# Pairwise field products on one core: five output slots that hold a whole tile, and five stores an inner tile in place of eleven

## The chip, the core and the metric

The kernel runs on one core of one Trainium2 chip. The metric is the device time of one execution in microseconds (us), and lower is better. TensorE (PE) multiplies into PSUM, VectorE (DVE), ScalarE (ACT) and GpSimd (POOL) work on the results, and SyncE (SP) issues nearly all DMAs, which 16 DMA engines carry out.

## The reference

For each of 2048 samples there are 32 fields of 64 float32 numbers, and for each of the 496 pairs of fields (i, j), i < j, a 64x64 matrix. The output of a pair is the projection of field i times field j, element by element:

```
PAIRS = np.array(list(combinations(range(NUM_FIELDS), 2)), dtype=np.int32)
...
xi = x[:, pi, :]
xj = x[:, pj, :]
proj = jnp.einsum('bpd,pod->bpo', xi, W)
return proj * xj
```

The output is 2048 x 496 x 64 float32, 260 MB. The inputs are 17 MB of x and some 8 MB of W.

## The kernel before

**Tiles.** The 2048 samples make 16 tiles of 128 samples, one sample to a partition. Tiles are numbered 0 to 15; 0 and 15 are written out apart, 1 to 14 are the inner tiles. In a tile a pair takes 64 columns, 256 bytes of each partition, 32 KB in all.

**Steps and groups.** `plan` cuts a tile into 21 steps. A step fills two PSUM units of up to 1024 columns, `proj[b][0]` and `proj[b][1]`, and `b` alternates between the two pairs of units. Steps are gathered in 11 groups, 0 to 10, each a contiguous run of output pairs: 61, 57, 53, 49, 45, 41, 37, 33, 54, 38 and 28 pairs. Groups 0 to 9 have two steps each, group 10 has one. Between step 9 (the last of group 4) and step 10 (the first of group 5) stands the "turn": PE transposes the x of the next tile into PSUM and ACT copies it into `x_t`.

**Engines.** PE projects (L288). DVE multiplies unit 0 by x straight out of PSUM into the output slot `staged` (L330), and for a third of the steps unit 1 too. For the other steps (`pool_steps`) ACT copies unit 1 into the slot (L254) and POOL multiplies it there in place (L228). PE may overwrite a unit when DVE or ACT has emptied it.

**Slots.** `staged` is a set of nine buffers in SBUF. Groups 0 to 8 have one each; group 9 shares the buffer of group 4, and group 10 that of group 5 (`SHARED_SLOTS`). Before DVE or ACT writes a group, `slot_free` waits until the last store out of its buffer has landed. For groups 0 to 8 that is a store of the tile before (of the same group, or for slots 4 and 5 of groups 9 and 10); for groups 9 and 10 it is the store of group 4 or 5 of the same tile.

**SP.** SP's program is a fixed order. For each tile it waits for each group in turn (the last unit emptied, and POOL done) and issues its store: 11 stores, L182. Then it issues the load of the x of the tile after next into the `x_sb` that this tile has just left (`load_x`, L187). This load stands in the queue behind all stores of the tile, and the turn of the next tile waits for it: the turn in tile t reads the x of tile t+1, which was asked for at the end of tile t-1. Tiles 14 and 15 issue no such load. All of these DMAs run through one queue on the same 16 engines, and a DMA of 128 rows gives each engine 8 rows and a semaphore write.

**Descriptor area.** The program is built with the default area of SBUF for DMA descriptors, 16 KB of each partition; no DMA of this kernel is issued by POOL, which is the engine that would use it.

Of the kernel before, what the change touches and what calls it, by code (L numbers as in the profile page):

```python
# [12 lines left out]
TURN_BEFORE = 10  # L13
WARM_UP = 16

SHARED_SLOTS = {9: 4, 10: 5}


def pair_index(i, j, fields):
# [51 lines left out]
def field_pair_project(nc, x, w, ident, out, fields, dim):  # L71
# [30 lines left out]
    slot_of = [SHARED_SLOTS.get(g, g) for g in range(len(groups))]  # L102
    slots = len(groups) - len(SHARED_SLOTS)
    assert sorted(set(slot_of)) == list(range(slots))
    slot_uses = [slot_of.count(k) for k in range(slots)]
    slot_pairs = [max(group_range(g)[1] for g in range(len(groups)) if slot_of[g] == k) for k in range(slots)]


    ends = {s: max(w_at[i] + (j - i - 1 + n) * dim for i, j, n in steps[s][0]) for s in range(len(steps))}
# [15 lines left out]
    with ExitStack() as ctx:  # L125
# [9 lines left out]

        x_t = [sb(f"x_t{h}", [P, fields // 2, P]) for h in range(2)]
        ident_sb = sb("ident_sb", [P, P])
        staged = [sb(f"staged{k}", [P, slot_pairs[k] * dim]) for k in range(slots)]
# [13 lines left out]

        block = ctx.enter_context(nc.Block())

        def slot_free(eng, tile, g):

            k = slot_of[g]
            before = [h for h in range(g) if slot_of[h] == k]
            if not (tile.first and not before):
                eng.wait_ge(stored[k], tile.number * 16 * slot_uses[k] + 16 * len(before))  # L160

        def staged_part(s, i, j, n):
            g = group_of[s]
            to = (pair_index(i, j, fields) - group_range(g)[0]) * dim
            return staged[slot_of[g]][:, to:to + n * dim]

        @block.sync
        def _(sp):
            def emit(tile):
                where = {item: (b, use) for item, b, use in items(tile)}  # L170
                for g, group in enumerate(groups):
                    first, n = group_range(g)


                    pooled = any(s in pool_steps for s in group)
                    if pooled and g == 0:
                        sp.wait_ge(pool_scaled[g], tile.number + 1)
                    b, use = where[group[-1]]
                    sp.wait_ge(emptied[b][group[-1] not in pool_steps], use + 1)
                    if pooled and g > 0:  # L180
                        sp.wait_ge(pool_scaled[g], tile.number + 1)  # L181
                    sp.dma_start(out[bass.ds(tile.number * P, P), first * dim:(first + n) * dim],  # L182
                                 staged[slot_of[g]][:, 0:n * dim]).then_inc(stored[slot_of[g]], 16)

            def load_x(tile):

                sp.dma_start(x_sb[tile.parity][:], x[bass.ds((tile.number + 2) * P, P), :]  # L187
                             ).then_inc(x_loaded[tile.parity], 16)

            half = fields * dim // 2  # L190
            sp.dma_start(x_sb[0][:, 0:half], x[0:P, 0:half]).then_inc(x_first_loaded[0], 16)
            sp.dma_start(w_sb[:, w_cuts[0]:w_cuts[1]], w[:, w_cuts[0]:w_cuts[1]]).then_inc(w_loaded[0], 16)
            sp.dma_start(x_sb[0][:, half:], x[0:P, half:]).then_inc(x_first_loaded[1], 16)
# [12 lines left out]
            with sp.Fori(0, (tiles - 4) // 2) as t:  # L206
                for tile in (Tile(2 * t + 1, 1, t), Tile(2 * t + 2, 0, t + 1)):
                    emit(tile)
                    load_x(tile)
            tile = Tile(tiles - 3, 1, tiles // 2 - 2)  # L210
            emit(tile)
            load_x(tile)
            emit(Tile(tiles - 2, 0, tiles // 2 - 1))
            emit(Tile(tiles - 1, 1, tiles // 2 - 1, last=True))
            for k in range(slots):
                sp.wait_ge(stored[k], 16 * slot_uses[k] * tiles)

        @block.gpsimd
        def _(pool):
# [16 lines left out]
        @block.scalar  # L236
        def _(act):
            act.dma_start(ident_sb[:], ident).then_inc(ident_loaded, 16)

            def turned_out(b, use, to):  # L240
                for h in range(2):
                    act.wait_ge(filled[b][h], use + 1)
                    nc.scalar.activation(x_t[to][:, h * (UNIT // P):(h + 1) * (UNIT // P), :].rearrange(  # L243
                        "p k b -> p (k b)"), proj[b][h][:], ACT.Copy).then_inc(emptied[b][h], 1)

            def emit(tile):
                for item, b, use in items(tile):
                    if item == "turn":
                        turned_out(b, use, 1 - tile.parity)
                    elif item in pool_steps:  # L250
                        (i, j, n), = steps[item][1]
                        slot_free(act, tile, group_of[item])
# [61 lines left out]
        @block.vector  # L314
        def _(dve):
            def emit(tile):
                if tile.first:
                    for h in range(2):
                        dve.wait_ge(x_first_loaded[h], 16)
                for item, b, use in items(tile):  # L320
                    if item == "turn":
                        continue
                    slot_free(dve, tile, group_of[item])
                    for h in range(2):
                        if h and item in pool_steps:
# [40 lines left out]
```

## Time and profile before

| | |
|---|---|
| time, median of 3 runs | 692.61 us (691.69 to 692.86) |
| the profiled execution | 691.5 us, of which the span of instructions is 689.7 us |
| PE, DVE, POOL, ACT busy | 595.4, 415.0, 390.7, 205.1 us |
| queue 1 (SP's) busy, share of 16 engines | 99.1% |
| moved | 285.16 MB, of it 260.05 MB written to HBM |
| mean granted TensorE clock | 0.904 of full speed |

How to read it: a busy time is the sum of an engine's instructions. The DMA share is the mean busy share of the 16 DMA engines, so one engine alone shows as 0.06. Since packets of a DMA engine can overlap, a stretch can show a little over 1. A DMA's time to landing runs from its issue to the semaphore that says all 16 engines are done. The granted clock has two levels, 1.00 (2.4 GHz) and 0.50 (1.2 GHz), and a stretch's value is their mean.

### The profile page before, as it was taken

The numbers are of one execution on the slowest core, as the hardware profiler recorded it, in microseconds if no ns is written. First come the engines' busy times: TensorE is split into PE (matmuls) and PEld (weight loads), VectorE is DVE, ScalarE is ACT, GpSimd is POOL, SyncE is SP. The second block draws the span as 40 slices with busy tenths as digits, with TensorE's granted clock in tenths as the row PEclk, the third lists the DMA queues.
The fourth block names the chain that finished last, engine by engine and source line by source line (L and its number), as shares of the span: only waits on it lengthen the run. The fifth ranks groups of instructions, "written<-read, shape, count | busy, mean of one in ns | idle before, by whom it ended". The sixth has DMA issues, their size and how long they took to land.

```text
span 689.7 us, 8297 instructions
## 1 busy us (share of the span) xinstructions
PE 595.4 (86%) x2704; PEld 370.3 (54%) x2704; DVE 415.0 (60%) x528; ACT 205.1 (30%) x257; POOL 390.7 (57%) x228
## 2 busy tenths in 40 slices
PE   6969979799797979979799797979979799797972
PEld 4636646465464646646466464645646466464541
DVE  1657647486574756646576574756647576474851
ACT  2412414233241422414233241422414224141320
POOL 0735737556473745738557474755728557374651
PEclk9988989899898997989989898998979989898995
DMA  8999999999999999999999999999999999999897
GB/s 341 398 427 425 430 428 426 426 422 428 420 427 427 419 426 394 425 421 416 428 402 429 409 430 426 412 424 411 425 425 378 422 409 424 414 431 425 362 419 310
DMA packets 29755, 285.16 MB, mean 413 GB/s; under 512 B 3312, under 2 KB 3440, under 8 KB 7216
## 3 DMA queue, kind: packets, MB, share of 16 engines
q1 hardware_dynamic: 29600, 284.96, 99.1%
q8 instruction: 5, 0.08, 0.0%
q10 hardware_dynamic: 144, 0.07, 0.0%
q14 instruction: 6, 0.05, 0.0%
HBM read 24.97 MB, written 260.05 MB: 413 GB/s over the span
## 4 chain that ended last, share of the span: by engine, by line
DMA 37%; POOL 26%; issue 22%; PE 10%; ACT 2%; DVE 1%; POOLq 0%; SPq 0%; DVEq 0%; ACTq 0%
DMA out_dram<-staged 36%; POOL staged L228 26%; PE proj L288 9%; ACT staged L254 2%; DVE staged L330 1%; DMA ident_sb<-ident_dram 1%; PE proj L305 1%; POOLq L227 0%; PE proj L266 0%; ACT x_t L243 0%; SPq L182 0%; POOLq L120 0%; ACTq L253 0%; DVEq L125 0%; SPq L181 0%
## 5 line engine op out<-in xcount | busy, mean ns | idle before, releaser
L288 PE MATMUL proj<-w_sb,x_t 64*128 64x512 f32 (+7 forms) x2432 | 561.8, 563 | 75.6 <-DVE staged L330 73.2
L330 DVE TENSOR_TENSOR staged<-proj,x_sb 128x1024 f32<-128x1024 f32 (+7 forms) x528 | 415.0, 828 | 263.8 <-PE proj L288 183.0
L228 POOL TENSOR_TENSOR staged<-staged,x_sb 128x1024 f32<-128x1024 f32 (+4 forms) x224 | 390.5, 1755 | 283.9 <-ACT staged L254 283.2
L288 PEld LDWEIGHTS proj<-w_sb,x_t 64*128 64x128 f32 x2432 | 338.4, 205 | 291.8 <-issue 134.1
L254 ACT ACTIVATE staged<-proj 128x1024 f32<-128x1024 f32 (+4 forms) x224 | 172.8, 787 | 455.5 <-PE proj L288 344.0
L243 ACT ACTIVATE x_t<-proj 128x1024 f32<-128x1024 f32 x32 | 31.0, 1021 | 10.6 <-PE proj L266 9.1
L266 PEld LDWEIGHTS proj<-ident_sb,x_sb 128*128 128x128 f32 x256 | 28.6, 143 | 8.8 <-issue 7.6
L266 PE MATMUL proj<-ident_sb,x_sb 128*128 128x128 f32 x256 | 32.2, 280 | 0.6 <-DMA x_sb<-x_dram 0.6
L305 PE MATMUL proj<-ident_sb 128*128 128x128 f32 x16 | 3.7, 421 | 5.5 <-DMA ident_sb<-ident_dram 5.5
L305 PEld LDWEIGHTS proj<-ident_sb 128*128 128x128 f32 x16 | 3.3, 223 | 5.5 <-DMA ident_sb<-ident_dram 5.5
L243 ACT ACT_TABLE_LOAD x1 | 1.3, 1283 | 1.2 <-PEq L360 1.2
L360 POOL MEMSET const-float32-0.0<- 128x1 f32 x1 | 0.1, 98 | 0.2 <-issue 0.2
L360 POOL MEMSET const-bfloat16-1.0<- 128x1 bf16 x1 | 0.1, 102 | 0.0
L360 POOL MEMSET const-uint8-127<- 128x1 uint8 x1 | 0.1, 102 | 0.0
L360 POOL MEMSET const-float32-1.0<- 128x1 f32 x1 | 0.1, 98 | 0.0
## 6 DMA issues: line engine op xcount, KB each, us to landing
out_dram<-staged SPq DMA_DIRECT2D x16, 1952.0 KB, 11.4
out_dram<-staged SPq DMA_DIRECT2D x16, 1824.0 KB, 14.1
out_dram<-staged SPq DMA_DIRECT2D x16, 1728.0 KB, 17.3
out_dram<-staged SPq DMA_DIRECT2D x16, 1696.0 KB, 14.7
out_dram<-staged SPq DMA_DIRECT2D x16, 1568.0 KB, 14.3
out_dram<-staged SPq DMA_DIRECT2D x16, 1440.0 KB, 15.6
out_dram<-staged SPq DMA_DIRECT2D x16, 1312.0 KB, 15.6
out_dram<-staged SPq DMA_DIRECT2D x16, 1216.0 KB, 12.1
```

Source lines behind the costliest of these rows:

```text
L228: last = nc.gpsimd.tensor_tensor(product, product, x_sb[tile.parity][:, j * dim:(j + n) * dim], ALU.mult)
L243: nc.scalar.activation(x_t[to][:, h * (UNIT // P):(h + 1) * (UNIT // P), :].rearrange("p k b -> p (k b)"), proj[b][h][:], ACT.Copy).then_i ...
L254: nc.scalar.activation(staged_part(item, i, j, n), proj[b][1][:, 0:n * dim], ACT.Copy).then_inc(emptied[b][1], 1)
L266: last = nc.tensor.transpose(proj[b][h][:, n * P:(n + 1) * P], x_sb[of][:, k * P:(k + 1) * P], ident_sb[:])
L288: last = nc.tensor.matmul(proj[b][h][:, at:at + width], x_t[tile.parity][half, i // 2, :], w_sb[half, col:col + width], start=True, stop=True)
L305: nc.tensor.transpose(proj[1][0][:, 0:P], ident_sb[:], ident_sb[:])
L330: last = nc.vector.tensor_tensor(staged_part(item, i, j, n), proj[b][h][:, at:at + n * dim], x_sb[tile.parity][:, j * dim:(j + n) * dim], ...
L360: nc = bacc.Bacc("TRN2", target_bir_lowering=False, num_devices=1)
```

## The change

There are now five slots, one for each of the merged runs of groups 0-1, 2-3, 4-6, 7-8 and 9-10, of 118, 102, 123, 87 and 66 pairs: 496 pairs, a whole tile, where the nine buffers held 430. No slot is used twice in a tile. The room comes from the descriptor area, cut to 1 KB of each partition.

In tiles 1 to 14 SP issues one store for each merged run, when its last group is done. Tiles 0 and 15 keep their eleven stores of one group each, which read their part of the slot. DVE and ACT wait for a slot once, at its first step (ACT: its first pool step), until the store of the tile before has landed; tile 0 waits for none, and tile 1 waits until all groups of a slot of tile 0 have landed.

```
+MERGED = [[0, 1], [2, 3], [4, 5, 6], [7, 8], [9, 10]]
+
+DMA_SCRATCH = 1024
...
+        staged = [sb(f"staged{k}", [P, n * dim]) for k, (_, n) in enumerate(slot_range)]
...
+        def slot_free(eng, tile, k):
+
+            if not tile.first:
+                eng.wait_ge(stored[k], tile.number * 16 + 16 * (len(MERGED[k]) - 1))
...
+                fine = tile.first or tile.last
+                for these in ([[g] for g in range(len(groups))] if fine else MERGED):
+                    k, g = slot_of[these[0]], these[-1]
+                    first, n = group_range(these[0])[0], sum(group_range(h)[1] for h in these)
...
+                    at = (first - slot_range[k][0]) * dim
                     sp.dma_start(out[bass.ds(tile.number * P, P), first * dim:(first + n) * dim],
-                                 staged[slot_of[g]][:, 0:n * dim]).then_inc(stored[slot_of[g]], 16)
+                                 staged[k][:, at:at + n * dim]).then_inc(stored[k], 16)
...
@@ -320,7 +324,9 @@
-                    slot_free(dve, tile, group_of[item])
+                    k = slot_of[group_of[item]]
+                    if item == groups[MERGED[k][0]][0]:
+                        slot_free(dve, tile, k)
...
+    nc = bacc.Bacc("TRN2", target_bir_lowering=False, num_devices=1,
+                   dynamic_dma_scratch_size=DMA_SCRATCH)
```

SP's program in the first tile of the loop, before: the stores of groups 0 to 8, their widths in float32 columns of a row (64 to a pair). Register instructions stand between them.

```order
L182 DMA out_dram<-staged 128x3904
L179 REGISTER_ALU
L182 ISA
L182 DMA out_dram<-staged 128x3648
L179 REGISTER_ALU
L182 ISA
L182 DMA out_dram<-staged 128x3392
L179 REGISTER_ALU
L182 ISA
L182 DMA out_dram<-staged 128x3136
```

And the same tile on SP now, from its first store to the load of x; `pool_scaled1` is POOL's signal for group 1 and `emptied` that of DVE or ACT.

```order
L184 DMA out_dram<-staged 128x7552
L180 REGISTER_ALU
L184 ISA [waits pool_scaled3,emptied00]
L184 DMA out_dram<-staged 128x6528
L180 REGISTER_ALU
L184 ISA [waits pool_scaled6,emptied10]
L184 DMA out_dram<-staged 128x7872
L180 REGISTER_ALU
L184 ISA [waits pool_scaled8,emptied11]
L184 DMA out_dram<-staged 128x5568
```

Two stores now take the place of the first four, a third that of groups 4, 5 and 6, and the load of x still comes behind the last store of the tile.

ACT's program around the turn in a tile of the loop, before (`stored` is a slot's semaphore, `filled` PE's; the two L243 rows are the copies of the turn):

```order
L253 REGISTER_ALU [waits stored4]
L254 ACTIVATE staged<-proj 128x896 [waits filled01]
L243 ACTIVATE x_t<-proj 128x1024 [waits filled10]
L243 ACTIVATE x_t<-proj 128x1024 [waits filled11]
L253 REGISTER_ALU [waits stored5]
L254 ACTIVATE staged<-proj 128x512 [waits filled01]
L253 REGISTER_ALU [waits stored6]
L254 ACTIVATE staged<-proj 128x512 [waits filled01]
L254 ACTIVATE staged<-proj 128x640 [waits filled11,stored6]
```

and the same rows now:

```order
L257 REGISTER_ALU [waits stored2]
L258 ACTIVATE staged<-proj 128x896 [waits filled01]
L245 ACTIVATE x_t<-proj 128x1024 [waits filled10]
L245 ACTIVATE x_t<-proj 128x1024 [waits filled11]
L257 REGISTER_ALU
L258 ACTIVATE staged<-proj 128x512 [waits filled01]
L257 REGISTER_ALU
L258 ACTIVATE staged<-proj 128x512 [waits filled01]
L258 ACTIVATE staged<-proj 128x640 [waits filled11]
```

The order of the work is the same; the waits for slots 5 and 6 are gone, and one wait, for the merged slot 2, stands ahead of step 9.

## Rows read from the trace of the kernel before

**Rows 1.** The page: span, DMA queue, busy engines and DMA share in 40 slices.

```profile
span 689.7 us, 8297 instructions
...
PE 595.4 (86%) x2704; PEld 370.3 (54%) x2704; DVE 415.0 (60%) x528; ACT 205.1 (30%) x257; POOL 390.7 (57%) x228
...
DMA  8999999999999999999999999999999999999897
...
q1 hardware_dynamic: 29600, 284.96, 99.1%
```

**Rows 2.** DMA issues of the page: count, KB each, median us from issue to landing.

```profile
out_dram<-staged SPq DMA_DIRECT2D x16, 1952.0 KB, 11.4
...
out_dram<-staged SPq DMA_DIRECT2D x16, 1728.0 KB, 17.3
...
out_dram<-staged SPq DMA_DIRECT2D x16, 896.0 KB, 10.5
```

**Rows 3.** Waits, whole run: total us, times, longest.

```profile
ACT staged L254 <- DMA out_dram<-staged: 111.0, 16, 9.0
...
DVE staged L330 <- DMA out_dram<-staged: 76.8, 16, 6.9
```

**Rows 4.** The chain: start, length of the pieces that end with group 4 landed.

```profile
77.22 15.10 DMA out_dram<-staged
...
616.24 15.57 DMA out_dram<-staged
```

**Rows 5.** Stretches: start:end, length, busy per engine, granted clock, DMA share, GB/s.

```profile
640.00:644.00 4.00, 4.00 (x22) 2.70 (x20) 3.02 (x3) 1.94 (x2) 2.82 (x2) 1.00 0.88 366
644.00:646.00 2.00, 2.00 (x11) 1.09 (x8) 2.00 (x3) 0.81 (x1) 2.00 (x2) 1.00 0.06 24
646.00:684.00 38.00, 26.75 (x117) 15.92 (x114) 20.46 (x29) 8.00 (x11) 19.48 (x12) 0.81 1.00 418
684.00:686.00 2.00, 0.00 (x0) 0.00 (x0) 0.00 (x0) 0.00 (x0) 0.00 (x0) 0.50 0.48 198
686.00:688.00 2.00, 0.00 (x0) 0.00 (x0) 0.00 (x0) 0.00 (x0) 0.00 (x0) 0.50 0.08 34
```

**Rows 6.** DMA queue 1 in 12:20, 71:88 and 88:98: packets, MB, share.

```profile
q1 hardware_dynamic: 668, 3.33, 101.6%
...
q1 hardware_dynamic: 597, 7.25, 100.3%
...
q1 hardware_dynamic: 481, 4.23, 99.8%
```

**Rows 7.** SP in order of time, 0:120, then group 6 with 7 (window 84:86).

```profile
0.75 0.40 SPq L191 DMA_DIRECT2D x_sb<-x_dram  x1
...
20.47 38.80 SPq L182 DMA_DIRECT2D out_dram<-staged  x11
59.32 0.46 SPq L187 DMA_DIRECT2D x_sb<-x_dram  x1
65.44 34.87 SPq L182 DMA_DIRECT2D out_dram<-staged  x11
...
84.67 1.47 SPq L182 DMA_DIRECT2D out_dram<-staged  x2
```

**Rows 8.** PE in order of time in tile 1; L266 is the turn.

```profile
73.81 1.97 PE L266 MATMUL proj<-ident_sb,x_sb 128*128 128x128 f32 x16
75.70 13.73 PE L288 MATMUL proj<-w_sb,x_t 64*128 64x512 f32 x64
93.38 15.00 PE L288 MATMUL proj<-w_sb,x_t 64*128 64x448 f32 x58 [3.94 <-DVE staged L330]
```

**Rows 9.** Stretches of the run's start and around tile 1's idle time.

```profile
0.00:5.00 5.00, 0.00 (x0) 0.00 (x0) 0.00 (x0) 1.28 (x1) 0.20 (x4) 1.00 0.56 150
...
89.00:92.00 3.00, 0.43 (x2) 0.00 (x0) 0.00 (x0) 0.00 (x0) 0.00 (x0) 1.00 1.00 426
92.00:95.00 3.00, 1.62 (x2) 0.83 (x3) 1.55 (x2) 1.19 (x2) 1.80 (x2) 0.59 1.01 429
95.00:98.00 3.00, 3.00 (x14) 2.68 (x14) 0.60 (x2) 0.00 (x0) 0.96 (x1) 0.50 1.01 427
98.00:101.00 3.00, 3.00 (x14) 1.61 (x12) 2.65 (x8) 0.38 (x1) 0.00 (x0) 0.78 1.02 434
```

More of the change, by code:

```diff
@@ L14 @@
 WARM_UP = 16
-SHARED_SLOTS = {9: 4, 10: 5}
+MERGED = [[0, 1], [2, 3], [4, 5, 6], [7, 8], [9, 10]]
+DMA_SCRATCH = 1024
 def pair_index(i, j, fields):
@@ L100, in group_range @@
         return first, sum(n for _, _, n in segments)
[L102 to L106, printed above, removed]
+    slot_of = [next(k for k, merged in enumerate(MERGED) if g in merged) for g in range(len(groups))]
+    slots = len(MERGED)
+    slot_range = [(group_range(m[0])[0], sum(group_range(g)[1] for g in m)) for m in MERGED]
     ends = {s: max(w_at[i] + (j - i - 1 + n) * dim for i, j, n in steps[s][0]) for s in range(len(steps))}
@@ L137, in field_pair_project @@
         ident_sb = sb("ident_sb", [P, P])
-        staged = [sb(f"staged{k}", [P, slot_pairs[k] * dim]) for k in range(slots)]
+        staged = [sb(f"staged{k}", [P, n * dim]) for k, (_, n) in enumerate(slot_range)]
         proj = [[ctx.enter_context(nc.psum_tensor(f"proj{b}{h}", [P, UNIT], F32)) for h in range(2)]
@@ L153, in field_pair_project @@
         block = ctx.enter_context(nc.Block())
[L155 to L160, printed above, removed]
+        def slot_free(eng, tile, k):
+            if not tile.first:
+                eng.wait_ge(stored[k], tile.number * 16 + 16 * (len(MERGED[k]) - 1))
         def staged_part(s, i, j, n):
-            g = group_of[s]
-            to = (pair_index(i, j, fields) - group_range(g)[0]) * dim
-            return staged[slot_of[g]][:, to:to + n * dim]
+            k = slot_of[group_of[s]]
+            to = (pair_index(i, j, fields) - slot_range[k][0]) * dim
+            return staged[k][:, to:to + n * dim]
         @block.sync
@@ L170, in emit @@
                 where = {item: (b, use) for item, b, use in items(tile)}
[L171 to L181, printed above, removed]
+                fine = tile.first or tile.last
+                for these in ([[g] for g in range(len(groups))] if fine else MERGED):
+                    k, g = slot_of[these[0]], these[-1]
+                    first, n = group_range(these[0])[0], sum(group_range(h)[1] for h in these)
+                    pooled = [h for h in these if any(s in pool_steps for s in groups[h])]
+                    if pooled and these[0] == 0:
+                        sp.wait_ge(pool_scaled[pooled[-1]], tile.number + 1)
+                    b, use = where[groups[g][-1]]
+                    sp.wait_ge(emptied[b][groups[g][-1] not in pool_steps], use + 1)
+                    if pooled and these[0] > 0:
+                        sp.wait_ge(pool_scaled[pooled[-1]], tile.number + 1)
+                    at = (first - slot_range[k][0]) * dim
                     sp.dma_start(out[bass.ds(tile.number * P, P), first * dim:(first + n) * dim],
-                                 staged[slot_of[g]][:, 0:n * dim]).then_inc(stored[slot_of[g]], 16)
+                                 staged[k][:, at:at + n * dim]).then_inc(stored[k], 16)
             def load_x(tile):
@@ L215, in _ @@
             for k in range(slots):
-                sp.wait_ge(stored[k], 16 * slot_uses[k] * tiles)
+                sp.wait_ge(stored[k], 16 * (tiles - 2 + 2 * len(MERGED[k])))
         @block.gpsimd
@@ L251, in emit @@
                         (i, j, n), = steps[item][1]
-                        slot_free(act, tile, group_of[item])
+                        k = slot_of[group_of[item]]
+                        if item == min(s for s in pool_steps if slot_of[group_of[s]] == k):
+                            slot_free(act, tile, k)
                         act.wait_ge(filled[b][1], use + 1)
@@ L322, in emit @@
                         continue
-                    slot_free(dve, tile, group_of[item])
+                    k = slot_of[group_of[item]]
+                    if item == groups[MERGED[k][0]][0]:
+                        slot_free(dve, tile, k)
                     for h in range(2):
@@ L359 @@
     }
-    nc = bacc.Bacc("TRN2", target_bir_lowering=False, num_devices=1)
+    nc = bacc.Bacc("TRN2", target_bir_lowering=False, num_devices=1,
+                   dynamic_dma_scratch_size=DMA_SCRATCH)
     aps = [nc.dram_tensor(n, a.shape, F32, kind="ExternalInput").ap() for n, a in arrays.items()]
```

## The prediction, made before the changed kernel was run

> **What bounds the kernel now.** I read the page first. The DMA queue is busy for 99.1% of the span, and all 40 slices but the first, the last and one near the end show a 9, while the busiest compute engine, PE, has 86% [rows 1]. So the kernel is bound by its transfers, and the question about any edit is what it does to the DMA engines' own time. Next, the waits. ACT and DVE each wait once a tile for a store to land, 111.0 and 76.8 us in 16 waits [rows 3]: compute is ahead and stands still until the shared buffer of group 9 is free. That waiting is a result of the bound and its removal is worth nothing by itself.
>
> Then the chain of waits, which has one long DMA piece a tile. It ends where group 4's store lands: at 77.22 + 15.10 = 92.32 us in tile 1 and at 616.24 + 15.57 = 631.81 in tile 14 [rows 4]. So a tile takes 539.49 / 13 = 41.50 us. It moves 496 pairs and one x, as much as 528 pairs of 32 KB, 17.30 MB.
>
> The stretches near the end say which DMA engine that is. At 644 to 646 us the DMA share is 0.06, one engine of 16: fifteen had run out of work and one had not. After the last work of the others the same is seen, 0.48 and then 0.08 [rows 5]. One engine is behind, and since a store has landed only when all 16 are done, that one sets the slots' release and the end. For it the queue isn't empty at any time that the rows show.
>
> **What a packet costs.** Three undisturbed stretches with rows of different length give it [rows 6]. Queue 1's busy time is share x 16 x length: 130.0 us for 668 packets (195 ns each, 4985 bytes) in 12:20, 272.8 us for 597 (457 ns, 12144 bytes) in 71:88, 159.7 us for 481 (332 ns, 8794 bytes) in 88:98. Each two of the three give a line: 0.0366, 0.0373 and 0.0361 ns a byte, and 12.0, 3.9 and 15.0 ns a packet whatever its size. I take their mean, about 10 ns, and keep 3.9 and 15 as bounds. As a check, a tile for an average engine: 17.30 MB / 16 x 0.0366 = 39.6 us, plus 12 DMAs x 9 packets (8 rows and a semaphore) x 10 ns = 1.1 us, 40.7 us in all. The 41.50 us of the chain are the slow engine's; 0.8 us a tile are its own.
>
> **The change, part by part.**
>
> Fewer stores. Tiles 1 to 14 issue 5 stores in place of 11, so 14 x 6 = 84 stores go, and with each 9 packets on every engine; the bytes stay. The slow engine saves 84 x 9 x 10 ns = 7.6 us (2.9 us at 3.9 ns, 11.3 at 15). All of it lies on the path, because that engine has no gap. SP's issuing of 84 stores goes too, and is worth nothing: SP waits for compute.
>
> On this the Trainium skill speaks twice (DMA: Bandwidth & Descriptors). Its Rules for kernel authors ask for 128 partitions and at least 1 MiB a DMA; all stores but that of group 10 (896 KB) fulfil it already [rows 2], and who stops there gets nothing for the merging. Its section Why small descriptors are slow gives a packet about three cycles of 32 bytes and 32 bytes of descriptor, 128 bytes in all; at 0.0366 ns a byte that is an estimate of 4.7 ns a packet and 3.6 us for the change. The rows above give a greater sum, so the trace does not agree with the size.
>
> The slow engine's 0.8 us a tile. No row says whether it pays them by bytes or by rows. By bytes nothing changes, and that is what I take, since the other 39.6 of its 41.5 us go by bytes too. By rows, 48 of 96 go and so does half: 0.4 x 14 = 5.6 us more gain. If long rows are dearer for it, it loses instead; a like amount the other way, up to 0.5 us a tile, 7 us, is my bound above.
>
> Slots. Each slot's use is a whole tile apart, so groups 9 and 10 wait for nothing of their own tile and the stall of rows 3 goes from its place. Compute doesn't get further ahead by much, since the next thing is late: the turn. The turn in tile t needs the x issued at the end of tile t-1, behind all of that tile's stores. Before, it never waited noticeably: in tile 1 it ran at 73.81 [rows 8] with x issued at 59.32 [rows 7]. Now compute is some groups further ahead when the queue reaches that x, so I expect PE to wait at the turn in each of tiles 1 to 14. Behind that wait stands everything of PE, and so groups 5 to 10 on all engines.
>
> Coarser issue. What covers this wait is what is already in the queue when x lands: merged runs 0 and 1 of the tile, 118 + 102 = 220 pairs. Group 4 is computed but can't be issued, since its run ends with group 6. At the new pace, 41.0 us for 528 pairs, the cover is 17.1 us. Within that time the turn, group 5 and group 6 must be done. In tile 1 before, from the turn's start at 73.81 [rows 8] to the issue of group 6 at 84.67 [rows 7] it took 10.9 us, all at clock 1.00 (2.4 GHz). After a stall of 3.9 us PE restarted at 93.38 [rows 8] and was granted 0.50 (1.2 GHz) until about 99.3, 5.9 us [rows 9]. Half of these 5.9 us is lost, so the way takes 10.9 + 3.0 = 13.9 us. From issue to first packet I allow 1.4 us: SP's first DMA issued at 0.75 [rows 7], and a share of 0.56 over the first 5 us [rows 9] means packets from 2.2 us on. 13.9 + 1.4 = 15.3 us against 17.1: the DMA engines don't run dry, with 1.8 us to spare. This is the thinnest number here. Once run 2 is issued there are 123 pairs of it, 9.6 us, to cover groups 7 and 8, and the rest of the tile is looser still.
>
> Other places cost nothing. A merged run 0 in tile 1 is issued later than group 0 was, but the stores of tile 0 cover it: the store of group 0 of tile 0 was issued at 20.47 and x at 59.32 [rows 7], and the queue was then busy to 71 us and beyond. Without the wait of group 9, tile 0 is done some 8 us sooner. At the end, tile 15 has its fine stores and group 10's as the last, as before, and one engine that ends after the others.
>
> **The sum.** The profiled execution took 691.5 us; less 7.6 gives 683.9. It lies 1.1 us under the median of 692.61, so the forecast for a median is 692.6 - 7.6 = **685.0 us**.
>
> **Rivals.**
>
> 1. The turn's wait isn't covered, slower. The place is the way from the turn to the issue of run 2, and the mechanism the granted clock. For it: there are 1.8 us to spare, and after every stall the clock was 0.50 for about 6 us; in the turn the small transposes may keep it there longer. Were it low on the whole way, 10.9 us of PE's work would take up to 21.7. From 17.1 - 1.4 = 15.7 us on, each us costs 14 us, so at 16.3 us the change is as slow as before (14 x 0.6 = 8.4 eats the gain of 7.6). With the clock low for 12 us the way takes 16.9 and the time is 692.6 - 7.6 + 14 x 1.2 = 702 us. Against it: in rows 9 the clock came back in full while PE had much to do, which holds behind the turn as well. Chance 0.08.
>
> 2. The slow engine pays by rows: 692.6 - 7.6 - 5.6 = 679.4 us. Chance 0.09.
>
> 3. Long rows are dearer for the slow engine. Its 0.8 us grow by 0.5 a tile, 7 us, and the time is 692.0, no change. For it: rows of up to 31 KB are twice as long as any in the trace. Against it: the three stretches lie on nearly one line from 5 to 12 KB. Chance 0.07.
>
> 4. The change doesn't do what it says. Rows over 16 KB are cut in two, so the packets come back and only the 84 semaphore writes go, 84 x 10 ns = 0.8 us: 691.8 us, no change. Nothing in the trace shows a row cut, but the longest is 15.6 KB. The Trainium skill's ≥1 MiB rule would give the same, by another way: a store's cost is amortized already. Against that stands the 10 ns line of rows 6. Chance 0.06.
>
> **How the numbers follow.** The forecast has 0.70, with its own range of 681.3 to 689.7 from the bounds of a packet. The range that holds 8 in 10 takes in the case of 679.4 and the edge of the forecast's upper side, 679.0 to 690.5; outside are 702, the two cases near 692 and a little of the rest. A measurement of this kernel tells 0.2%, 1.4 us, from no change. Faster by more than that is everything under 691.2: 0.70 + 0.09, and a little of cases 3 and 4, **0.80**. Within 0.2%: **0.12**. Slower: **0.08**.
>
> **What would show it.** Right: queue 1 has 84 x 144 = 12096 packets fewer, 17504 in place of 29600; from one tile to the next 41.0 us in place of 41.50; ACT and DVE no longer wait for a store in each tile, and PE waits about 4 us at the turn for the load of x, with clock 0.50 behind it; the DMA share stays at 0.98 or more, and at the end one engine is left alone. Wrong: a DMA share that falls once a tile to 0 between run 1 and run 2 (rival 1), a period under 40.7 us (rival 2), or 41.5 us with the fewer packets (rival 3) or as many packets as before (rival 4). If 84 stores less take off under 3 us with no dip in the share, the 10 ns of a packet were wrong.

## The result, and the profile after

The changed kernel is slower. Its median is 696.74 us (6 runs, 695.55 to 698.52) against 691.79 us for the kernel before (6 runs on the same chip, 691.28 to 692.86): a ratio of 1.0071, 95% interval 1.0061 to 1.0081. The forecast was 685.0 us, faster. The profiled execution took 697.26 us with a span of 695.5.

The page of the changed kernel has these rows; the last two parts are the chain by engine and the DMA issues (count, KB each, median us from issue to landing):

```profile
span 695.5 us, 7741 instructions
...
PE 577.8 (83%) x2704; PEld 364.4 (52%) x2704; DVE 410.6 (59%) x528; ACT 208.5 (30%) x257; POOL 391.6 (56%) x228
...
DMA  8999999999999999999999999999999999999997
...
q1 hardware_dynamic: 17504, 284.96, 98.9%
...
PE 44%; DMA 43%; DVE 6%; SPq 2%; issue 1%; ACT 0%; DVEq 0%; ACTq 0%
...
x_sb<-x_dram SPq DMA_DIRECT2D x15, 1024.0 KB, 19.6
```

The 12096 packets are gone, exactly as forecast, and the bytes are the same. The queue is as busy as before, 98.9% against 99.1% [rows 1], and its 40 slices show nothing. By this view the kernel has fewer packets, the same bytes and the same busy share, and yet takes longer. So the time of some packets must have grown.

The waits (total us, times, longest) show where compute stands now:

```profile
ACT x_t L245 <- PE proj L270: 114.2, 31, 7.9
...
PE proj L270 <- DMA x_sb<-x_dram: 83.0, 15, 6.2
```

No wait for a store is left on ACT or DVE; those of rows 3 are gone. In their place PE waits at the turn for x, 5.5 us on average, as forecast (about 4). The chain of waits (start, length) gives the period from one turn to the next:

```profile
53.80 18.20 DMA x_sb<-x_dram
72.05 3.68 PE proj L270 x16
...
178.30 19.56 DMA x_sb<-x_dram
197.90 3.67 PE proj L270 x16
...
618.02 3.68 PE proj L270 x16
```

(618.02 - 72.05) / 13 = 42.00 us a tile, where 41.50 was measured before [rows 4] and 41.0 was forecast. In the chain the load of x now stands where group 4's store stood.

Last, stretches (columns as in rows 5) behind one turn, and at the end of the run:

```profile
197.00:211.00 14.00, 12.84 (x55) 8.62 (x57) 6.02 (x8) 4.42 (x6) 4.07 (x3) 0.76 0.98 420
...
665.00:689.00 24.00, 5.52 (x32) 3.72 (x29) 5.76 (x11) 1.43 (x3) 4.89 (x3) 0.71 1.01 424
689.00:692.00 3.00, 0.00 (x0) 0.00 (x0) 0.00 (x0) 0.00 (x0) 0.00 (x0) 0.50 0.79 327
692.00:695.50 3.50, 0.00 (x0) 0.00 (x0) 0.00 (x0) 0.00 (x0) 0.00 (x0) 0.50 0.07 29
```

Behind the turn the granted clock is 0.76 on average for 14 us, and the DMA share is 0.98: what was feared there, a queue that runs empty, hardly happens.

### The profile page after: what moved, and what is told of

The parts are those of the page before. It is cut to its first block, busy times and chain, and to the rows that moved or that the text cites. A ratio compares the mean times of both kernels' runs of the same rounds, so it can differ in the third digit from the quotient of the medians.

```text
span 695.5 us, 7741 instructions
## 1 busy us (share of the span) xinstructions
PE 577.8 (83%) x2704; PEld 364.4 (52%) x2704; DVE 410.6 (59%) x528; ACT 208.5 (30%) x257; POOL 391.6 (56%) x228
## 3 DMA queue, kind: packets, MB, share of 16 engines
q1 hardware_dynamic: 17504, 284.96, 98.9%
## 4 chain that ended last, share of the span: by engine, by line
PE 44%; DMA 43%; DVE 6%; SPq 2%; issue 1%; ACT 0%; DVEq 0%; ACTq 0%
DMA x_sb<-x_dram 43%; PE proj L292 37%; PE proj L270 8%; DVE staged L336 6%; SPq L197 1%; SPq L184 1%; SPq L189 0%; ACT staged L258 0%; SPq L201 0%; SPq L195 0%; SPq L194 0%; SPq L193 0%; DVEq L333 0%; DVEq L126 0%; ACTq L257 0%
## 5 line engine op out<-in xcount | busy, mean ns | idle before, releaser
L336 DVE TENSOR_TENSOR staged<-proj,x_sb 128x1024 f32<-128x1024 f32 (+7 forms) x528 | 410.6, 827 | 261.9 <-PE proj L292 259.3
L292 PE MATMUL proj<-w_sb,x_t 64*128 64x512 f32 (+7 forms) x2432 | 521.0, 536 | 4.0 <-DVE staged L336 2.6
L292 PEld LDWEIGHTS proj<-w_sb,x_t 64*128 64x128 f32 x2432 | 311.9, 190 | 207.8 <-issue 126.7
L270 PE MATMUL proj<-ident_sb,x_sb 128*128 128x128 f32 x256 | 54.4, 401 | 83.0 <-DMA x_sb<-x_dram 83.0
L270 PEld LDWEIGHTS proj<-ident_sb,x_sb 128*128 128x128 f32 x256 | 49.2, 215 | 92.2 <-DMA x_sb<-x_dram 92.2
L245 ACT ACTIVATE x_t<-proj 128x1024 f32<-128x1024 f32 x32 | 32.6, 1024 | 114.2 <-PE proj L270 114.2
## 6 DMA issues: line engine op xcount, KB each, us to landing
out_dram<-staged SPq DMA_DIRECT2D x14, 2112.0 KB, 17.1
out_dram<-staged SPq DMA_DIRECT2D x2, 1952.0 KB, 16.1
```

The costliest lines, as they stand in the source:

```text
L270: last = nc.tensor.transpose(proj[b][h][:, n * P:(n + 1) * P], x_sb[of][:, k * P:(k + 1) * P], ident_sb[:])
L292: last = nc.tensor.matmul(proj[b][h][:, at:at + width], x_t[tile.parity][half, i // 2, :], w_sb[half, col:col + width], start=True, stop=True)
L336: last = nc.vector.tensor_tensor(staged_part(item, i, j, n), proj[b][h][:, at:at + n * dim], x_sb[tile.parity][:, j * dim:(j + n) * dim], ...
```

## Experiments

The studies ran with before beside them each time; its median was 691.55 to 691.89 us. "Ratio" is to before, with its 95% interval. Each diff is against the changed kernel unless it says otherwise.

### Is the saving there, and what does x cost?

Two kernels load no x inside the run, one made from the changed kernel and one from before. Tiles 2 to 15 are computed from old values of x; the loads are left out, nothing else.

```
             def load_x(tile):
-                sp.dma_start(x_sb[tile.parity][:], x[bass.ds((tile.number + 2) * P, P), :]
-                             ).then_inc(x_loaded[tile.parity], 16)
+                return
...
                     if item == "turn":
-                        pe.wait_ge(x_loaded[1 - tile.parity], 16 * tile.half + 16)
+                        if tile.first:
+                            pe.wait_ge(x_loaded[1], 16)
```

> The changed kernel without the loads of x in tiles 0 to 13 (the turn uses the x that is there; this leaves 14 MB of transfers out, so the output is of stale samples). Both theories put the loss at the load of x, in the half-speed packets around it: 696.7 less 14 x 2.4 us of x and less 14 x 1.5 us of half speed is about 642 us, and 7 us less than the kernel before without its loads. Rival C (long rows are dearer everywhere, or the engines run dry between merged runs): the difference to the kernel before without its loads stays +5 us.

> The kernel before without the loads of x in tiles 0 to 13 (stale samples, 14 MB of transfers left out). 692 less 14 x 2.4 us is 658 us; if the half-speed packets around x cost it 0.4 us a tile too, 652. The packets' fixed cost says it is 7 us slower than the changed kernel without x loads; rival C says 5 us faster.

Measured: 652.97 us (0.9444, 0.9428 to 0.9460) for the changed kernel, 658.66 us (0.9523, 0.9507 to 0.9539) for before. The views of DMA queues of the first and of the second:

```profile
q1 hardware_dynamic: 15488, 270.28, 97.6%
```

```profile
q1 hardware_dynamic: 27584, 270.28, 98.4%
```

Without x, the change is worth 5.7 us. For 84 stores of 9 packets that is 7.5 ns a packet, where the forecast took 10. So the saving is real, and it is lost at x. Before pays 691.87 - 658.66 = 33.2 us for 14 loads, 2.37 us each; their 14.68 MB at the 427 GB/s of an undisturbed stretch would take 34.4 us, so it pays the bytes and no more. The changed kernel pays 696.74 - 652.97 = 43.8 us, **10.6 us more for the same loads**. Before was expected at 658 us, and the changed kernel at 642, 11 us too low: that took off 1.5 us of slow packets a tile beside the 2.4 us of x, where a load is worth 43.8 / 14 = 3.1 us in all.

### Is it the slots, the long rows, or the form of x?

All stores fine again, in slots of a whole tile:

```
+STORES = [[0], [1], [2], [3], [4], [5], [6], [7], [8], [9], [10]]
...
-                for these in ([[g] for g in range(len(groups))] if fine else MERGED):
+                for these in ([[g] for g in range(len(groups))] if fine else STORES):
```

> The changed kernel with its five whole-tile slots, but eleven stores in every tile, so only the slots differ from before (and the place where compute waits, the turn). Theory A (long rows: what the change lost comes from the merged stores, whose long rows stand next to the load of x): the time is that of before, 691 to 693 us, and packets of x take 309 ns in the median and near it in the mean. Theory B (the slots: compute waits for x at the turn, the queue is deeper when x is read, and the packets around the load of x take up to double their time for that reason): the half-speed packets stay, about 1.5 us a tile, and with the 7 us of packets back the time is 702 to 704 us.

Measured 694.96 us (1.0046, 1.0029 to 1.0063), between what the two theories gave. So 3.1 us of the loss come with the slots (and the smaller descriptor area, which was not tried apart), with not one store merged; merging on top of them, which should have brought 7.6, added 1.8.

The rows of x in device memory 9 KB apart in place of 8:

```
-        "x_dram": np.ascontiguousarray(r_x).reshape(batch, fields * dim),
+        "x_dram": np.pad(np.ascontiguousarray(r_x).reshape(batch, fields * dim), ((0, 0), (0, 256))),
```

> The changed kernel with the rows of x in HBM 9 KB apart in place of 8 KB (256 unused columns at the end of each row; the same bytes are moved). Theory D (the 16 engines read rows a power of two apart and meet in the same part of HBM, which halves their rate): the packets of x go back to 309 ns and the time falls by up to 14 x 1.5 = 21 us, to 676 us or a part of the way. Theories A and B: no change, 696 to 698 us.

Measured 697.0 us (1.0063, 1.0044 to 1.0081), the time of the changed kernel. The pitch of x's rows has no part in it.

The run ahead of x split, so that a short row stands before x as it did before:

```
+STORES = [[0, 1], [2, 3], [4, 5, 6], [7, 8], [9], [10]]
```

> The changed kernel with the last merged run stored as its two groups again (9, then 10: six stores an inner tile), so that rows of 7 KB stand ahead of the load of x in place of 17 KB. Theory A (the row length next to x sets what it costs): the slow packets ahead of x shrink and the time falls to between that of the kernel with all stores fine (695.0, which has 5.9 us more of packets) and 690 us. Theory B (the slots and the place of the wait alone set it): one store more a tile costs 1.2 us, 697.9 us.

Measured 696.74 us (1.0070, 1.0053 to 1.0086): no change. The length of the rows just ahead of x changes the time by no more than the 1 us that the one store more a tile may hide.

x in two halves, with the last store between them, which doubles the changes between storing and loading:

```
+                    if these[-1] == 8 and loads:
+                        sp.dma_start(x_sb[tile.parity][:, 0:half], x[bass.ds((tile.number + 2) * P, P), 0:half]
+                                     ).then_inc(x_lower[tile.parity], 16)
...
-                sp.dma_start(x_sb[tile.parity][:], x[bass.ds((tile.number + 2) * P, P), :]
+                sp.dma_start(x_sb[tile.parity][:, half:], x[bass.ds((tile.number + 2) * P, P), half:]
```

> The changed kernel with x loaded in two halves of 4 KB rows, fields 0 to 15 ahead of the last run's store and fields 16 to 31 behind it: the same bytes, but four changes between loading and storing a tile in place of two. If the cost of x goes by the number of such changes (10.5 us for 14 x 2), it doubles: 707 us. If it goes by the bytes of x it stays at 697 to 698 us (one DMA more a tile, 1.2 us). If it comes from compute waiting for a late x, the turn's first half starts 7 us earlier and the time falls.

Measured 695.2 us (1.0046, 1.0032 to 1.0060), 1.5 us less and not more. A fixed price for each change of direction is out.

### Is it x's place in the queue?

ACT issues the load, in a queue of its own, after the first step of the next tile; the same for before and for the kernel with fine stores.

```
-            def load_x(tile):
-                sp.dma_start(x_sb[tile.parity][:], x[bass.ds((tile.number + 2) * P, P), :]
-                             ).then_inc(x_loaded[tile.parity], 16)
...
+                    if item == 0 and not (tile.first or tile.last):
+                        for h in range(2):
+                            act.wait_ge(emptied[0][h], tile.number * per_tile + 1)
+                        act.wait_ge(pool_scaled[9], tile.number)
+                        act.dma_start(x_sb[1 - tile.parity][:], x[bass.ds((tile.number + 1) * P, P), :]
+                                      ).then_inc(x_loaded[1 - tile.parity], 16)
```

> The changed kernel with the loads of x issued by ACT on its own queue in the next tile's first step, so that x does not stand behind the stores and its packets mix with theirs. x lands well ahead of the turn, PE does not wait there, and each engine takes rows of both queues in turn. If the cost lies in x standing in line behind long stores and ahead of them (and in the wait at the turn): about 653.0 + 14 x 2.4 = 686.7 us. If reading and writing at the same time is what halves the rate, every row of x pays and takes store rows with it: above 700 us.

> The kernel before with the loads of x on ACT's queue in the same way. Before, x cost no more than its bytes (33.2 us for 14 x 2.4), so moving it can gain nothing by the first theory: 691 to 693 us, and the changed kernel's version is 5 to 6 us faster. By the second it goes above 700 us too.

> Whole-tile slots, eleven stores a tile and x on ACT's queue. Against 686.2 us with five stores a tile it has 84 stores more: if the slots and the merging are independent once x is out of the line, 686.2 + 7.0 = 693 us. If the slots themselves still cost 3 us there, 696.

Measured: 686.2 us (0.9922, 0.9906 to 0.9939) for the changed kernel, 692.98 us (1.0013, 1.0004 to 1.0023) for before, 691.3 us (0.9999, 0.9989 to 1.0008) for the fine stores. The changed kernel gains 10.5 us by it, just what its x costs more, and before loses 1.1. With x out of the way, merging is worth 691.3 - 686.2 = 5.1 us and the whole change 692.98 - 686.2 = 6.8 us, 9.0 ns a packet. So the cost arises where x stands in one line with the stores: 10.5 us in the changed kernel, 694.96 - 691.3 = 3.7 us with the fine stores in its slots, none in the kernel before. What is different had to be found.

### Is it the wait at the turn, or what is queued behind x?

The turn three groups later (before step 16), so that groups 5 to 7 don't stand behind the wait for x:

```
-TURN_BEFORE = 10
+TURN_BEFORE = 16
```

> The changed kernel with the turn six steps later in a tile (behind step 15, the end of group 7, in place of step 9), x still in line behind the stores. PE reaches the turn some 13 us later, so it waits little or not at all for x. If compute's wait at the turn (and its restart at the lower clock) is what costs the 10.5 us: the time falls to about 686 us. If x in line between the stores costs it, whatever compute does: it stays at 696 to 697 us and the slow packets around x remain.

And from the kernel before, with its shared buffers, three merges where these allow it:

```
+RUNS = [[0, 1], [2, 3], [4], [5], [6], [7, 8], [9], [10]]
+
-SHARED_SLOTS = {9: 4, 10: 5}
+SHARED_SLOTS = {6: 2, 7: 3}
```

> The kernel before with its own slot sharing (groups 9 and 10 in the buffers of 4 and 5), only that groups 0-1, 2-3 and 7-8 are stored in one DMA each, in all tiles: 8 stores a tile in place of 11, 48 fewer in all. The turn does not wait, as before. By the packets alone 48 x 0.084 = 4.0 us less, 687.9 us. If merging costs more around x whatever the slots are: 691 us or more.

Measured 688.6 us (0.9954, 0.9937 to 0.9970) and 688.78 us (0.9960, 0.9946 to 0.9974). The second shows that merging pays in the old scheme: 48 stores fewer bring 2.8 us, 6.4 ns a packet. The first regains 8.1 us by one number, and lies between the 686 us and the 696 that its two theories gave. But the wait itself is not what was costly. It is nearly as long as it was, 64.6 us in 14 against 83.0 in 15:

```profile
PE proj L270 <- DMA x_sb<-x_dram: 64.6, 14, 5.7
```

What differs is how much is queued when x lands. In order of time, PE at the turn and then SP's next store (start, length):

```profile
361.57 3.68 PE L270 MATMUL proj<-ident_sb,x_sb 128*128 128x128 f32 x16 [5.29 <-DMA x_sb<-x_dram]
```

```profile
371.61 0.33 SPq L184 DMA_DIRECT2D out_dram<-staged  x1
```

Runs 0 to 2 are in the queue when x lands, 343 pairs, and 10.0 us later the next store is issued. That gave a theory to test.

### The theory of the short lead, and two kernels that price it

The stores behind x are all that an engine can do until run 2 is issued. An engine that is through with x and with runs 0 and 1 must wait there. So the fast engines can be ahead of the slowest by no more than the work in the queue less the way to the next issue. In the changed kernel that is little: the 16 engines are held together, they all come to x at the same time, and that is when packets are slow. To test it, give group 4 back its own store (265 pairs queued in place of 220), and put the turn one group earlier (the way gets longer).

```
+STORES = [[0, 1], [2, 3], [4], [5, 6], [7, 8], [9, 10]]
```

> The changed kernel with group 4, which is computed ahead of the turn, in a store of its own (groups 0-1, 2-3, 4, 5-6, 7-8, 9-10: six stores an inner tile). When x lands, 265 pairs are in the queue in place of 220, 3.5 us more. Six stores as in the kernel with the last run split (696.7 us), so the packets are the same. Theory H (the engines are held together: run 2 is issued some 15 us after x has landed on the slowest engine, with 17.1 us of work behind x, so no engine can be more than 2.5 us ahead of the slowest, all meet the slow stretch around x at once, and the slowest pays it too): with 6 us of room the slowest engine is left out of it as before, and the time falls to 688 to 691 us. Theory S (the merged rows or the slots slow the loads of x by themselves): 696 to 697 us.

```
-TURN_BEFORE = 10
+TURN_BEFORE = 8
```

> The changed kernel with the turn two steps earlier (behind step 7), so that group 4 too stands between x's landing and the issue of run 2. The way from x's landing to that issue grows by two steps, about 3.5 us, against the same 17.1 us of cover. Theory H: the 2.5 us of room become 1 us too little; the slowest engine now runs dry once a tile, and the time is 696.7 + 14 x 1 = 710 us, with a visible dip of the DMA share once a tile. Theory S: 696 to 698 us.

Measured 691.09 us (0.9985, 0.9974 to 0.9995) and 708.26 us (1.0235, 1.0215 to 1.0254), where the theory had put 688 to 691 and 710 us; the other theory, that the slots or the long rows slow the loads by themselves, had put 696 to 698 for both. One store *more* in each tile made the kernel 5.7 us faster, with its wait at the turn left almost as it was, 74.6 us in 15:

```profile
PE proj L273 <- DMA x_sb<-x_dram: 74.6, 15, 6.0
```

The lead can be read from rows such as these, the turn and the next store that depends on it, of the changed kernel, of the one with group 4's own store and of the one with the earlier turn:

```profile
367.24 3.68 PE L270 MATMUL proj<-ident_sb,x_sb 128*128 128x128 f32 x16 [6.00 <-DMA x_sb<-x_dram]
```

```profile
379.45 0.33 SPq L184 DMA_DIRECT2D out_dram<-staged  x1
```

```profile
361.61 3.67 PE L273 MATMUL proj<-ident_sb,x_sb 128*128 128x128 f32 x16 [4.34 <-DMA x_sb<-x_dram]
```

```profile
374.57 0.33 SPq L187 DMA_DIRECT2D out_dram<-staged  x1
```

```profile
329.96 3.67 PE L270 MATMUL proj<-ident_sb,x_sb 128*128 128x128 f32 x16 [6.25 <-DMA x_sb<-x_dram]
```

```profile
346.06 0.33 SPq L184 DMA_DIRECT2D out_dram<-staged  x1
```

The table works with the prediction's own terms: 0.0777 us a pair (41.0 us for 528) and 1.4 us from issue to first packet. Its last column is the time less that of the twin with x on the second queue. The row of the fine stores goes by their group 5, issued at 372.67 us, 8.7 us after the turn at 363.95. For group 4's own store no twin was run; its twin is put at 686.2 + 14 x 9 x 10 ns = 687.5 (an estimate); for the kernels that differ in the turn alone, the changed kernel's 686.2 is used.

| kernel | queued when x lands, pairs (us) | way to the next issue + 1.4, us | lead, us | over its twin, us |
|---|---|---|---|---|
| turn before step 16 | 343 (26.6) | 11.4 | 15.2 | 2.4 |
| fine stores | 265 (20.6) | 10.1 | 10.5 | 3.7 |
| group 4's own store | 265 (20.6) | 14.4 | 6.2 | 3.6 |
| changed | 220 (17.1) | 13.6 (in tile 4: 14.7) | 3.5 (2.4) | 10.5 |
| turn before step 8 | 220 (17.1) | 17.5 | -0.4 | 22.1 |

In these kernels, all with the slots of a whole tile, the price grows as the lead shrinks: it is nearly level down to a lead of 6 us and steep below. Even the kernel with fine stores, whose x PE waits for as well, pays 3.7 us at x; on the second queue it is 1.7 us faster than before's twin (691.3 against 692.98), so the 3.1 us that the slots cost lie at x too, and the small descriptor area, which this kernel has as well, costs nothing that can be seen. Two more views follow, and the packets themselves.

**At the end of the run** one can see how far the engines are apart: how long one of them, a share of 0.06, is left alone. The columns are those of rows 5. First the turn before step 8, then the changed kernel's two rows above, then group 4's own store, then the turn before step 16, then x on the second queue, and last no x at all:

```profile
700.00:703.00 3.00, 0.00 (x0) 0.00 (x0) 0.00 (x0) 0.00 (x0) 0.00 (x0) 0.50 1.00 417
703.00:706.00 3.00, 0.00 (x0) 0.00 (x0) 0.00 (x0) 0.00 (x0) 0.00 (x0) 0.50 0.46 192
```

```profile
684.00:687.00 3.00, 0.00 (x0) 0.00 (x0) 0.00 (x0) 0.00 (x0) 0.00 (x0) 0.50 0.06 27
```

```profile
678.00:681.00 3.00, 0.00 (x0) 0.00 (x0) 0.00 (x0) 0.00 (x0) 0.00 (x0) 0.50 0.20 86
681.00:685.00 4.00, 0.00 (x0) 0.00 (x0) 0.00 (x0) 0.00 (x0) 0.00 (x0) 0.50 0.07 28
```

```profile
672.00:675.00 3.00, 0.00 (x0) 0.00 (x0) 0.00 (x0) 0.00 (x0) 0.00 (x0) 0.50 0.26 108
675.00:678.00 3.00, 0.00 (x0) 0.00 (x0) 0.00 (x0) 0.00 (x0) 0.00 (x0) 0.50 0.07 30
678.00:681.00 3.00, 0.00 (x0) 0.00 (x0) 0.00 (x0) 0.00 (x0) 0.00 (x0) 0.50 0.05 23
```

```profile
633.00:637.00 4.00, 0.00 (x0) 0.00 (x0) 0.00 (x0) 0.00 (x0) 0.00 (x0) 0.50 0.53 221
637.00:641.00 4.00, 0.00 (x0) 0.00 (x0) 0.00 (x0) 0.00 (x0) 0.00 (x0) 0.50 0.07 30
641.00:645.00 4.00, 0.00 (x0) 0.00 (x0) 0.00 (x0) 0.00 (x0) 0.00 (x0) 0.50 0.06 24
```

With the shortest lead, the engines end nearly together. In the changed kernel one is alone for at most 3.5 us. Without x one is alone from 637 us to 650. Where the others are free to run on, the slow engine alone sets the time. But the kernel before ends like the changed one (a share of 0.48, then 0.08 from 686 us on in a span of 689.7 [rows 5]): its engines are no further apart at the end, and it doesn't pay for it.

**Around x** the rate falls while the busy share doesn't. Stretches of 10 us around a load of x, first before, two tiles, and before with x on the second queue, two tiles; then the changed kernel, two tiles; then its variants: group 4's own store, turn before step 8, turn before step 16 (two tiles), and x on the second queue. The last two columns are DMA share and GB/s:

```profile
349.00:359.00 10.00, 10.00 (x49) 6.10 (x47) 8.40 (x8) 3.77 (x4) 6.92 (x4) 1.00 1.02 394
391.00:401.00 10.00, 10.00 (x49) 6.11 (x47) 8.39 (x9) 3.74 (x4) 7.67 (x4) 1.00 1.03 403
```

```profile
348.00:358.00 10.00, 10.00 (x48) 5.78 (x45) 8.85 (x13) 2.92 (x4) 6.22 (x3) 1.00 1.02 399
393.00:403.00 10.00, 10.00 (x49) 6.10 (x47) 8.39 (x9) 3.75 (x4) 7.69 (x4) 1.00 0.87 340
```

```profile
356.00:366.00 10.00, 5.24 (x24) 2.76 (x20) 4.79 (x6) 2.43 (x3) 7.55 (x4) 0.92 1.00 360
398.00:408.00 10.00, 5.27 (x24) 2.76 (x20) 4.81 (x6) 2.43 (x3) 7.58 (x4) 0.87 1.02 362
```

```profile
348.00:358.00 10.00, 9.26 (x41) 5.08 (x39) 8.49 (x10) 3.69 (x5) 7.58 (x5) 1.00 1.02 368
```

```profile
405.00:415.00 10.00, 4.11 (x22) 2.05 (x18) 3.81 (x5) 2.54 (x3) 5.99 (x4) 0.95 1.03 360
```

```profile
345.00:355.00 10.00, 9.75 (x43) 5.46 (x42) 7.24 (x11) 4.01 (x6) 8.28 (x6) 1.00 1.01 419
387.00:397.00 10.00, 10.00 (x47) 5.83 (x44) 7.94 (x10) 3.57 (x6) 9.13 (x6) 1.00 1.03 419
```

```profile
330.00:345.00 15.00, 14.35 (x65) 8.27 (x63) 10.10 (x10) 5.08 (x6) 11.71 (x6) 1.00 1.01 425
```

All but one of them show a share of 1.00 or more, so the engines hardly idle. But in the changed kernel they move 361 GB/s in place of some 427, so these 10 us hold 10 x (1 - 361 / 427) = 1.5 us of lost work for an average engine. Before it is 0.6 to 0.8, and moving its load to the second queue doesn't help: 399 GB/s in one tile and, with some idle time, 340 in the next. With the late turn, x stands in the same queue behind the same long stores, and there is next to nothing. In 2 us ahead of the turn of tile 4 the changed kernel had 292 GB/s, here with a share of 0.85:

```profile
190.00:192.00 2.00, 2.00 (x10) 1.03 (x6) 1.79 (x3) 0.00 (x0) 2.00 (x2) 1.00 0.85 292
```

Group 4's own store shows a limit of this view. There the rate falls too (368, and 389 over 390:400), and the time is still good. The rate is the mean of 16 engines and the time is that of the last one. By the theory the last one can come to x when the others are through with a lead of 6 us, and with 3 us it can't. This is argued from the times, not shown: no view tells which engine a packet belongs to.

**The rows of x one by one.** The traces hold the start and length of every packet, and those of x can be told by their 8192 bytes. These are the means over the 13 loads of x behind tiles 1 to 13; an undisturbed row takes 309 ns. "Apart" is the first column less 7 rows, an engine's own way from its first row to its last:

| kernel | first to last start of x's 128 rows, us | one row, ns | apart, us |
|---|---|---|---|
| turn before step 16 | 13.6 | 342 | 11.2 |
| fine stores | 10.4 | 384 | 7.7 |
| group 4's own store | 8.5 | 390 | 5.8 |
| changed | 6.6 | 435 | 3.6 |
| turn before step 8 | 4.5 | 457 | 1.3 |
| before | 7.5 | 330 | 5.2 |
| before with three merges | 6.3 | 337 | 3.9 |
| changed, x on the second queue | 10.5 | 309 | |

In the first five kernels the engines are apart in the order of the computed lead and close to it, and the rows of x get slower as it shrinks. The two kernels with the old slots don't fit: with three merges the engines come to x as close together as in the changed kernel, and the rows take 337 ns in place of 435. So a short lead alone doesn't make x slow. Something else that differs between the two families must play a part, and no run singles it out.

### Once x is out of the way

Three slots and three stores a tile, x on the second queue, the turn before step 10 and before step 16:

```
-MERGED = [[0, 1], [2, 3], [4, 5, 6], [7, 8], [9, 10]]
+MERGED = [[0, 1, 2, 3], [4, 5, 6], [7, 8, 9, 10]]
```

> x on ACT's queue and three slots of 220, 123 and 153 pairs, three stores an inner tile: 28 stores fewer than with five. By the packets 686.2 - 28 x 0.084 = 683.9 us. If the coarser slots make the engines run dry: above 687 us.

> The fastest version so far (three slots, three stores, x on ACT's queue, 685.2 us), where PE still waited at the turn for x (38 us in 14 waits), with the turn behind step 15. If the slowest engine alone sets the time there (it ran alone for the last 10 us and more), nothing changes: 685 us. If the wait at the turn cost anything: 683 to 684.

Measured 685.17 us (0.9907, 0.9891 to 0.9924) and 685.09 us (0.9906, 0.9889 to 0.9922); 683.9 had been expected of the first. 28 stores fewer bring another 1.0 us, 4.1 ns a packet, and the place of the turn is worth nothing any more. This is the fastest version found, 0.9% under before.

## Why the prediction was wrong

The forecast was a gain of 7.6 us; the change lost 4.9 to 5.0 us against the kernel before beside it. The median it started from (692.61 of three runs, against 691.79 of six) accounts for 0.8 us of the gap to 685.0 and no more.

**What bounds it.** Right: the transfers, and of the 16 engines one. With x out of the way, the time is what the slow engine needs, and the change brings nearly what was forecast.

**Fewer stores.** The term was right in kind and a little large: 7.6 us forecast; 5.7 without x, 6.8 with x on the second queue, 7.5 and 9.0 ns a packet, inside the bounds of 3.9 and 15. The merges tried alone gave 6.4 and 6.7 ns, the step from five stores to three 4.1. The Trainium skill's estimate in the prediction (DMA: Bandwidth & Descriptors, section Why small descriptors are slow) was 4.7 ns and 3.6 us; all but the last of these lie above it. The Trainium skill's rule of at least 1 MiB a DMA (the same page, Rules for kernel authors), read in the prediction as if merging beyond it brought nothing, is not borne out in that reading either: stores of 1.1 to 2 MB (all but group 10's, of 0.9) gained by being merged.

**Slots.** Right: the stall of rows 3 went and the wait at the turn came in its place, 5.5 us long in place of 4. As forecast, the wait in itself costs nothing, at least once x is on the second queue: of the two three-store kernels the one whose PE waits 37.9 us in 14 turns takes 685.17 us, and the one that doesn't wait there 685.09.

**Coarser issue.** This is the step that failed. Its numbers were good: a way of 13.9 us was forecast and 12.2 to 13.3 were taken, 17.1 us of work stood against them, and the share of 0.98 says that the queue hardly ran dry. The conclusion, that with 1.8 us to spare it costs nothing, was wrong: with 3.5 us more work queued behind x (group 4's own store) the kernel is 5.7 us faster, and with the late turn 8.1 us. The prediction asked whether the queue gets empty. By the theory above it should have asked how far the fast engines can get ahead. It had itself found that one engine sets the time and the others have slack, and then cut that slack to 3 us without pricing it. It also took x as a DMA like the others, at the price of its bytes. In before it is that, 2.37 us; in the changed kernel it is 43.8 / 14 = 3.13 us.

**Rival 1** named the place, the way from the turn to the issue of run 2, and a wrong mechanism: a way made long by the low clock, and dry engines from 15.7 us on. The way was shorter than that, and the loss was there all the same. Dry engines do come with a longer way. With the turn one group earlier the way is 16.1 us, without the 1.4 to the first packet, the share over the run is down, and in another tile two microseconds around the issue of run 2 at 431.53 us show it, at the full clock:

```profile
q1 hardware_dynamic: 17504, 284.96, 98.1%
```

```profile
430.00:432.00 2.00, 2.00 (x14) 1.25 (x13) 1.31 (x3) 0.60 (x1) 1.73 (x2) 1.00 0.28 118
```

Idle time there is 1.9% of 706.6 us, 13.4 us, against 1.1% of 695.5, 7.7 us. So of the 11.5 us that this kernel takes more than the changed one, some 6 are idle time of the average engine.

**Rivals 2 to 4.** Rows cut in two: no, 17504 packets. A gain or a loss of the slow engine by long rows: the 5.7 and 6.8 us leave 1 to 2 us for it at most, on the side of a loss, and don't tell it from a lower price of a packet.

**The signs that were named.** Packets, the turn's wait, the half clock behind it and the share above 0.98 came as said. One engine is left at the end too, as in before. The period did not come (42.0 in place of 41.0), and no sign named a period above 41.5. Only the variants tell what the end of the run means: with nothing in the way one engine is alone for 8 us (x on the second queue) or 13 (no x), so in the changed kernel the others were held back to it.

**What stays open** is why packets are slow around x in the kernels with whole-tile slots. It isn't the pitch of x's rows, the length of the row ahead, or the number of changes between storing and loading, each tried by itself. It isn't the engines' closeness alone either, since before with three merges has them as close and its rows of x take 337 ns. That more work behind x brings the time back is shown; that it does so through the lead is argued.

## What to carry to other kernels

A DMA share of 1.0 doesn't say that the transfers run at full rate: look at GB/s over share, around each load that stands in line with stores. When stores are merged, or a wait is put ahead of an issue, work out how much is queued against the way to the next issue, and ask not only whether it gets empty but whether several us are left, by which the fast DMA engines can lead the slowest; with the slots of a whole tile, 3 us left cost 10 us here and 6 us left cost 4. In the kernel that waits for its load, a queue of its own for the load cured it, and merging even large stores then brought its few nanoseconds a packet.

## What the runs showed of the hardware

In every run but that with the earliest turn, a single one of the 16 DMA engines was left at the end. Where nothing holds the others back it is alone for 13 us at the end of a 651 us run.

A packet of a row of 7 to 56 KB costs 4 to 9 ns beside its bytes, by the stores left out.

In the changed kernel, with stores and the load in one queue, the engines moved about 361 GB/s over 10 us around the load with a busy share of 1.00 to 1.02, and 292 over 2 us with 0.85. With the late turn, or with the load in another queue, the rate was 419 to 425 GB/s there. The kernel before had 394 and 403, and its load in another queue changed nothing for the better (399 and 340).

A row of x (8 KB) takes 309 ns undisturbed, 435 on average in the changed kernel, and 309 again with the load in another queue.
